# Layer 1's attention: stacks of even and odd heads on the two halves of the partitions, and their score products issued in twos

## The reference

```
q = x @ Wq; k = x @ Wk; v = x @ Wv            # 16 heads; 4 heads; 4 heads
q = rope(q); k = rope(k)
scores = einsum('bhqd,bhkd->bhqk', q, k) / sqrt(D)
p = softmax(scores); o = einsum('bhqk,bhkd->bhqd', p, v)
x = x + o @ Wo + slots_ffn(xn)                # slots: top-8 routing of 64 slots, a GRU step, slot values
```

## Time and profile before

| | us |
|---|---|
| median of 3 executions | 3566.41 (3564.4 to 3569.42) |
| profiled execution, its own time | 3567.51 |
| its span, first to last instruction | 3565.8 |
| TensorE busy | 3229.5 (91%) |
| VectorE busy | 1783.8 (50%) |
| ScalarE busy | 1356.0 (38%) |
| mean granted TensorE clock | 0.933 of full |

### The profile page before, as it was taken

How to read it: one execution, slowest core, us unless ns; L and a number is a source line. 1 busy time by engine, 2 the same in 40 slices (tenths; PEclk the granted TensorE clock), 3 DMA queues, 4 the chain that set the end, 5 groups by cost and what they waited for, 6 DMA issues and landing times.

```text
span 3565.8 us, 51313 instructions
## 1 busy us (share of the span) xinstructions
PE 3229.5 (91%) x15366; PEld 1977.2 (55%) x15367; DVE 1783.8 (50%) x3626; ACT 1356.0 (38%) x1937; POOL 378.9 (11%) x413
## 2 busy tenths in 40 slices
PE   6999999999998999999999999989998688988988
PEld 3455455545544555555545555447665466766666
DVE  5444444544445777777646555662223543334441
ACT  1533434344342555555543233322232233333333
POOL 1100001010000000000011111110111211111110
PEclk7899899889887999999999999989999799999999
DMA  7323422432402222222340101012212333333330
GB/s 230 102 88 85 125 89 61 124 95 68 129 23 75 57 56 56 56 56 56 87 161 30 45 32 40 31 42 69 100 63 66 87 77 84 83 83 76 80 84 14
DMA packets 133002, 273.03 MB, mean 77 GB/s; under 512 B 19680, under 2 KB 77472, under 8 KB 120896
## 3 DMA queue, kind: packets, MB, share of 16 engines
q1 hardware_dynamic: 120352, 233.29, 23.6%
q0 software_dynamic: 10464, 28.59, 2.7%
q10 hardware_dynamic: 2128, 10.43, 0.8%
HBM read 172.49 MB, written 104.33 MB: 78 GB/s over the span
## 4 chain that ended last, share of the span: by engine, by line
PE 77%; DVE 11%; issue 5%; ACT 4%; DMA 2%; POOL 1%; DVEq 0%; SPq 0%; ACTq 0%; POOLq 0%
PE bank_u L526 7%; PE pair L510 6%; PE bank L464 6%; PE bank L487 5%; PE pair L566 4%; PE pair L687 3%; PE pair L1863 3%; PE bank_m L464 3%; PE pair L2230 3%; PE pair L2603 3%; DVE nmax L850 3%; PE pair L731 2%; PE bank_m L2567 2%; PE bank L2567 2%; PE pair L475 2%
## 5 line engine op out<-in xcount | busy, mean ns | idle before, releaser
L763 ACT ACTIVATE probs<-pair 128x1024 f32<-128x1024 f32 x512 | 505.1, 1022 | 341.4 <-PE pair L510 338.3
L850 DVE TENSOR_REDUCE nmax<-bank 128x1 f32<-128x512 f32 x679 | 449.7, 684 | 260.6 <-PE bank L487 256.9
L526 PE MATMUL bank_u<-probs,vext 128*32 128x512 f32 x2048 | 288.2, 636 | 0.8 <-ACT probs L763 0.5
L850 DVE TENSOR_REDUCE nmax<-bank_m 128x1 f32<-128x512 f32 x345 | 235.9, 684 | 79.8 <-PE bank_m L487 74.3
L510 PE MATMUL pair<-q_a,k_a 98*128 98x512 f32 x512 | 192.4, 483 | 46.4 <-DVEq L905 23.6
L1956 DVE TENSOR_REDUCE nmax<-bank 128x2 f32<-128x512 f32 x177 | 118.2, 688 | 179.2 <-PE bank L1786 131.4
L487 PE MATMUL bank<-k_a,q_a 96*128 96x512 f32 x351 | 185.5, 571 | 9.2 <-DMA k_a<-parts_dram 8.4
L510 PEld LDWEIGHTS pair<-q_a,k_a 98*128 98x128 f32 x512 | 102.7, 224 | 142.2 <-ACT probs L763 62.0
L1895 ACT ACTIVATE probs<-pair 128x896 f32<-128x896 f32 x128 | 117.2, 917 | 143.2 <-PE pair L1804 142.3
L510 PE MATMUL pair<-q,k 98*128 98x512 f32 x512 | 167.7, 410 | 3.4 <-DVEq L1515 3.3
L487 PE MATMUL bank<-k,q 96*128 96x512 f32 x328 | 150.4, 493 | 19.8 <-DMA k<-parts_dram 10.7
(11 more groups left out here) (386 smaller groups left out, 6182.0 us busy)
## 6 DMA issues: line engine op xcount, KB each, us to landing
parts_dram<-parts SPq DMA_DIRECT2D x72, 512.0 KB, 2.8
q_a<-parts_dram SPq DMA_DIRECT2D x32, 512.0 KB, 5.1
k_a<-parts_dram SPq DMA_DIRECT2D x32, 512.0 KB, 6.8
q<-parts_dram SPq DMA_DIRECT2D x64, 256.0 KB, 3.7
xl<-xs SPq DMA_DIRECT2D x31, 512.0 KB
xres<-xs SPq DMA_DIRECT2D x24, 512.0 KB
xs<-xres SPq DMA_DIRECT2D x24, 512.0 KB, 3.0
x_in<-xg SPq DMA_DIRECT2D x74, 128.0 KB, 2.0
```

The costliest lines, as they stand in the source:

```text
L526: ins = nc.tensor.matmul(bank_u[32 * h:32 * h + 32, :], vext[:, kt, kv(g, h), :], probs[:, kt % 2, h * SEQ:(h + 1) * SEQ], start=(kt == 0) ...
L763: nc.scalar.activation(probs[:, kt % 2, hp * 2 * SEQ:hp * 2 * SEQ + n], st.tile(l, name)[:, 0:n], ACT.Exp).then_inc(st.free["act"].sem, 1)
L850: nc.vector.tensor_reduce(nmax[:, g % 2, qt, h:h + 1], sc.tile(l, name)[:], AX, ALU.max, negate=True).then_inc(sc.free["dve"].sem, 1)
```

## The change

Both the query and the key stacks now exist on two halves of the partitions. Even heads' stacks stand on partitions 0 to 47 with their maxima on 48 and 49, odd heads' on 64 to 111 with maxima on 112 and 113, and the keys are loaded to both halves. A product contracts 48 or 50 rows. The maxima's products are issued in twos, an even and an odd head of the same query tile: TensorE first waits for both banks, then issues both, and the second one signals for both. `pe_scores_t` keeps its order, but its two heads now lie on different halves. Zeroing the queries is no longer needed (four MEMSETs of VectorE in `POST0` go). A stack takes eight transfers of SP instead of four, and the load of a group's maxima rows two instead of one. `SHARE1` and `sc_plan1` move one product so that all counts are even. A spare tile keeps the addresses of what follows.

```diff
 def sc_plan1(front, back):
-                    ("back", s_uses(3)[:8] + m_use(2) + s_uses(3)[8:13]), ("front", [("L", "dve")]),
-                    ("back", turn_uses(0) + s_uses(3)[13:] + [("GX", "dve")]),
+                    ("back", s_uses(3)[:8] + m_use(2) + s_uses(3)[8:12]), ("front", [("L", "dve")]),
+                    ("back", turn_uses(0) + s_uses(3)[12:] + [("GX", "dve")]),
...
+        def score_at(l, i):
+            return (2 * (i // (2 * TT)) + i % 2, i // 2 % TT) if LAYER[l] == 1 else (i // TT, i % TT)
...
         def dve_max(dve, l, it, step, g, i):
-            h, qt = i // TT, i % TT
+            h, qt = score_at(l, i)
...
-                if not front:
-                    dve_clear_queries(dve, l, 2)
...
-            sp.dma_start(q_rows(g), m_dram[g].rearrange("(a h) n -> a h n", a=2)).then_inc(m_loaded[g % 2].sem, 16)
+            if LAYER[l] == 1:
+                for side in range(2):
+                    sp.dma_start(q_rows(g, side), m_dram[g].rearrange("(a h s) n -> s a h n", a=2, s=2)[side])\
+                      .then_inc(m_loaded[g % 2].sem, 16)
...
-        q_1 = sb("q_1", [P, GROUPS, GH, SEQ], F32, l1)
+        q_1 = sb("q_1", [P, GROUPS, GH // 2, SEQ], F32, l1)
+        spare_q = sb("spare_q", [P, 8 * SEQ], F32, l1)
...
-            nc.vector.memset(k_1[0:96, :, :], 0.0).then_inc(dve_pre1, 1)
-            nc.vector.memset(k_1[96:98, :, :], 1.0).then_inc(dve_pre1, 1)
+            for side in range(2):
+                nc.vector.memset(k_1[64 * side + 32:64 * side + 64, :, :], 1.0).then_inc(dve_pre1, 1)
...
-        def dve_clear_queries(dve, l, g):
-            dve.wait_ge(*st.filled(l, 0, ("E", g, TT - 1, 1)))
-            nc.vector.memset(q_1[0:96, g, :, :], 0.0).then_inc(queries_clear, 1)
...
-        SHARE1 = [6, 8, 10, 12, 13, 14, 15, 16, 16]
+        SHARE1 = [6, 8, 10, 12, 12, 14, 14, 16, 16]
...
             def pair(g, h):
-                return k_1[0:98, g, :], q_1[0:98, g, h, :]
+                at = h % 2 * 64
+                return k_1[at:at + 50, g, :], q_1[at:at + 50, g, h // 2, :]
+
+            def two_scores(g, first, last):
+                for i in range(first, last, 2):
+                    if i == 0:
+                        pe.wait_ge(*stack_ready(l, it, g))
+                    for j in range(2):
+                        for s in sc.vacated(l, it, ("S", g, i + j)):
+                            pe.wait_ge(*s)
+                    for j in range(2):
+                        h, qt = score_at(l, i + j)
+                        ins = nc.tensor.matmul(sc.tile(l, ("S", g, i + j))[:], q(g, h)[:, qt * P:(qt + 1) * P].bitcast(F32R),
+                                               k(g, h).bitcast(F32R), start=True, stop=True)
+                    ins.then_inc(sc.full.sem, 2)
...
                     def maxima(j):
                         if back if g < 2 else front:
-                            for i in range(cut[j], cut[j + 1]):
-                                pe_scores(pe, l, it, (g + 2) % GROUPS, i, q, k)
+                            two_scores((g + 2) % GROUPS, cut[j], cut[j + 1])
...
-                heads = slice(GH * g, GH * g + GH)
-                sp_stack(sp, l, it, g, 0, q_1[:, g, :, :], DIM, HD, heads)
-                sp_stack(sp, l, it, g, 1, k_1[:, g:g + 1, :], 64, HD, slice(g, g + 1))
+                for side in range(2):
+                    at = 64 * side
+                    sp_stack(sp, l, it, g, 0, q_1[at:at + 48, g, :, :], DIM, HD, slice(GH * g + side, GH * g + GH, 2))
+                    sp_stack(sp, l, it, g, 1, k_1[at:at + 48, g:g + 1, :], 64, HD, slice(g, g + 1))
```

More of the change, by code:

```diff
@@ L347, in build @@
         parts_stored = [sig(f"parts_stored{i}", [(16 * SLOT0.count(i), 0), (16 * (i < 3), 0), 0, (16, 0)], "sync") for i in range(4)]
-        stack_loaded = [sig(f"stack_loaded{g}", [(64, 0), (64, 0), 0, (64, 0)], "sync") for g in range(GROUPS)]
+        stack_loaded = [sig(f"stack_loaded{g}", [(64, 0), (128, 0), 0, (64, 0)], "sync") for g in range(GROUPS)]
         high_ready = sig("high_ready", [(8, 0), (3, 0), 0, (4, 0)], "scalar")
@@ L351, in build @@
         m_stored = sig("m_stored", [(16, 48), (16, 48), 0, (16, 48)], "sync")
-        m_loaded = [sig(f"m_loaded{i}", [(16 - 16 * i, 16 + 16 * i), (16 - 16 * i, 16 + 16 * i), 0, (16 - 16 * i, 16 + 16 * i)], "sync")
+        m_loaded = [sig(f"m_loaded{i}", [(16 - 16 * i, 16 + 16 * i), (32 - 32 * i, 32 + 32 * i), 0, (16 - 16 * i, 16 + 16 * i)], "sync")
                     for i in range(2)]
@@ L371, in max_rows_loaded @@
         def max_rows_loaded(l, it, g):
-            return m_loaded[g % 2].at(l, it, 16 * (g // 2 + 1) if g % 2 else 8 * g)
+            return m_loaded[g % 2].at(l, it, (2 if LAYER[l] == 1 else 1) * (16 * (g // 2 + 1) if g % 2 else 8 * g))
+        def score_at(l, i):
+            return (2 * (i // (2 * TT)) + i % 2, i // 2 % TT) if LAYER[l] == 1 else (i // TT, i % TT)
         def stack_ready(l, it, g):
@@ L939, in dve0 @@
                 if not front:
-                    dve_clear_queries(dve, l, 0)
                     dve_slots(dve, l)
@@ L955, in dve0 @@
                 if not front:
-                    dve_clear_queries(dve, l, 1)
                     dve_slot_gates(dve, l)
                 dve_normalise_heads(dve, l, it, step, 2)
-                if not front:
-                    dve_clear_queries(dve, l, 2)
             maxima(1, 0, 8)
@@ L965, in dve0 @@
             if back:
-                if not front:
-                    dve_clear_queries(dve, l, 3)
                 dve_add_out(dve, l, it)
@@ L1039, in sp_max_rows @@
             sp.wait_ge(*m_stored.at(l, it, 16 * (m_order(l, g) + 1)))
-            sp.dma_start(q_rows(g), m_dram[g].rearrange("(a h) n -> a h n", a=2)).then_inc(m_loaded[g % 2].sem, 16)
+            if LAYER[l] == 1:
+                for side in range(2):
+                    sp.dma_start(q_rows(g, side), m_dram[g].rearrange("(a h s) n -> s a h n", a=2, s=2)[side])\
+                      .then_inc(m_loaded[g % 2].sem, 16)
+            else:
+                sp.dma_start(q_rows(g), m_dram[g].rearrange("(a h) n -> a h n", a=2)).then_inc(m_loaded[g % 2].sem, 16)
         def sp_store_out(sp, l, it):
@@ L1202, in build @@
         N1B = 16 * (len(loads1b) + 1)
-        dve_set1, dve_pre1, queries_clear = sem("dve_set1"), sem("dve_pre1"), sem("queries_clear")
+        dve_set1, dve_pre1 = sem("dve_set1"), sem("dve_pre1")
         layer_left = [sem(f"layer_left{i}") for i in range(3)]
@@ L1224, in sp_setup1b @@
             sp.dma_start(bias_bc[:, 0, :], bc("bo1", DIM)).then_inc(loaded1b, 16)
-            sp.wait_ge(queries_clear, GROUPS)
         def pe_slots(pe, l):
@@ L1305, in q @@
             def q(g, h):
-                return q_1[0:96, g, h, :]
+                at = h % 2 * 64
+                return q_1[at:at + 48, g, h // 2, :]
             def k(g, h):
-                return k_1[0:96, g, :]
+                at = h % 2 * 64
+                return k_1[at:at + 48, g, :]
             def pair(g, h):
-                return k_1[0:98, g, :], q_1[0:98, g, h, :]
+                at = h % 2 * 64
+                return k_1[at:at + 50, g, :], q_1[at:at + 50, g, h // 2, :]
[11 more added lines that the diff above has]
+                    ins.then_inc(sc.full.sem, 2)
             def last_maxima(first, last):
                 if back:
-                    for i in range(first, last):
-                        pe_scores(pe, l, it, 3, i, q, k)
+                    two_scores(3, first, last)
             def project(name, half, weight, width=P, halves=2):
@@ L1630, in dve1 @@
             if back:
-                maxima(3, 9, 13)
+                maxima(3, 9, 12)
             if front:
@@ L1635, in dve1 @@
                 dve_normalise_heads(dve, l, it, step, 0)
-                maxima(3, 13, 16)
+                maxima(3, 12, 16)
             if back:
@@ L1678, in sp1 @@
             sp_rounds(sp, l, it, [(rows(0, DIM, 0, P), parts[:, 0, :, :]), (rows(0, DIM, P, P), parts[:, 1, :, :]),
-                                  (rows(1, 64, 0, 64), k_parts[:])], stack, lambda g: q_1[96:98, g, :, :])
+                                  (rows(1, 64, 0, 64), k_parts[:])], stack, lambda g, side: q_1[64 * side + 48:64 * side + 50, g, :, :])
         full.close()
```

## The result

The changed kernel is slower: 3610.7 us (median of 4 executions, 3591.6 to 3626.4) against 3567.9 (4, 3564.4 to 3571.2), a ratio of 1.012 [1.007, 1.017]. Four more executions, taken later beside other runs of before, have a median of 3606.7, 1.014 [1.011, 1.018]. The prediction was 3565.5, with a range from 3549 to 3590.

A forecast was written before the change was run, and what follows sets the result against it. TensorE streams nearly without a gap, but VectorE's banks set a step's start. Seven turns -6.3, PRE1 +6.6, its stack +1.0, POST0 -1.8, POST1 -0.4 sum to -0.9 us: 3566.6 profiled, median 3565.5, range 3549 to 3590.

The forecast's parts named there:

- the sum: Whole kernel: loop turns, PRE1 and its stack, POST0 and POST1 together change the time by -0.9 us.
- Rival (3): Group 2 of the loop: clock falls as less of the array works; 3577 to 3590 us, chance 0.15.
- rival (2): Loop: weight loads overlap, stack in time; step 2.8 us, a turn gains 2.3; total 3553, chance 0.25.
- Pair side by side: TensorE: two products on the array's two halves take 0.25 us together, against 0.47 before.
- Step: Loop, one weighing to the next: 3.0 us with two pairs, against 3.17 before.
- Turn: One turn of layer 1's loop gains 0.9 us: 1.3 in group 3 less 0.4 for the late stack.
- Borders: Loop: 22 new changes of array shape a turn at 0.2 us each, 4.4 us of TensorE's time.
- Double wait: Each maxima pair waits for two banks; the second is free 0.68 us after VectorE starts the pair's first maximum.
- PRE1: Before the loop, at half clock: a pair of maxima takes 1.73 us against 1.22, +6.6 us in all.
- Stack 0 in the loop: SP's queue: eight transfers land at 1358.7, so the product needing them starts 0.4 us later each turn.
- Rival (4): Array halves don't run side by side: step 3.55 us, loop +36, PRE1 +10; 3609 us, chance 0.10.
- rival (5): Loop: stack 0 lands late, +1.5 us a turn; 3576 us, chance 0.10.

The follow-up runs named there:

- e3_twowait: Kernel before, its maxima's products of 96 rows issued in twos behind a wait for both banks, one signal for both; 3616.9 us, ratio 1.015.
- e11_again: The changed kernel run once more, unaltered, in four later executions: median 3606.7 us, ratio 1.014 to the kernel before.
- e1_rows48: Kernel before, its products contracting 48 and 50 rows on one half of the partitions, one at a time; 3645.0 us, ratio 1.022.
- e8_pool0: e2_single with the four transfers of stack 0's odd half issued by GpSimd's queue instead of SP's; 3607.0 us, ratio 1.012.
- e2_single: Changed kernel, its maxima's products issued singly, each with its own bank wait and signal; halves and eight transfers kept; 3591.9 us, ratio 1.009.

## Why the prediction was wrong

**The failed step is the sum, which costed every turn at the full clock.** The sum was -0.9 us; measured are +24 in the profiled executions and +43 at the medians. It had no term for the clock, and the time at half clock grew: by 99 us in the profiled executions, by about 140 at the medians. Rival (3) did name the mechanism and the place, group 2, but set 0.15 on it with one argument against it, "all turns are at 1.00 now though group 2 waits". That says only that waiting with 98 rows does not lower the clock (e3_twowait shows the same). The prediction's own sign for it, a clock below 1.00 in group 2, is what the trace shows. The size was short as well: one or two stretches of 5 us a turn, against 7 to 14 us at half clock in the last six turns of the profiled run and up to 20 in e11_again.

What a microsecond at half clock costs can be read from turns of one kernel. e1_rows48: 45.3 us for 0.39 x 2 x 134.3 = 105, 0.43 each. The changed kernel: 2.44 for 2 x (0.08 x 89.9 - 0.04 x 87.5) = 7.4, 0.33. e8_pool0's two turns above give 0.32, e2_single's 0.50. (The prediction used 1.7 for 5 us, or 0.34 each.) The mean clock fell from 0.933 to 0.914 at the median: 2 x (0.086 x 3609 - 0.067 x 3566) = 143 us more at half clock, at 0.4 each +57. Measured are +43. So everything else, by this estimate, gave 14 us back, where rival (2), 3553, had 12. With 0.32 to 0.50 it is 3 to 29 us, so the agreement is no proof. That the change would win at a held clock is argued from these numbers, and no run shows it: none held the clock without paying for it.

**The other steps.** *Pair side by side*, 0.25 taken: 0.33 to the next instruction, right in kind and a little short; the weight loads overlap too, which the prediction left open. *Step*: 3.0 predicted, 2.94 to 2.96. *Turn*: -0.9 predicted at the full clock; 87.5 less 7 x 0.4 is 84.7 as an estimate, -2.3, which is rival (2)'s figure. *Borders*: 22 counted at 4.4 a turn, +1.9 in e1_rows48, presumably since VectorE's work covers many. *Double wait*: it costs a turn 4.6 with products one behind the other (e3_twowait). With pairs the step of group 3 is 2.94 with it and without it. Over the whole kernel e2_single's ratio is 0.2 to 0.5% under the changed one's, with intervals that touch; clear is only `PRE1`, 6 us. *PRE1*: two pairs in a row,

```profile
1108.80 0.76 PE L1325 MATMUL bank_m<-k,q 48*128 48x512 f32 x1 [0.88 <-DVE nmax L854]
...
1110.47 0.76 PE L1325 MATMUL bank<-k,q 48*128 48x512 f32 x1 [0.88 <-DVE nmax L854]
```

This is 1.67 a pair against 1.73 predicted. From the first product to the first instruction behind the maxima (L1352; L1338 in the kernel before) it is 29.2 instead of 22.8, +6.4 for +6.6 predicted, and 23.2 with single issue. *PRE1's stack*: +1.0 predicted, it came 2.8 earlier, since the whole chain of splits and stores stands 1.5 earlier in `PRE1` and the loads land sooner. *Stack 0 in the loop*: +0.4 predicted. Counted from the turn's start, the first product of group 0 stands 0.9 later in the turn from 1320.87 and 2.5 later in the quick turns, of which a wait for the stack is 0.6; in e2_single's long turns it is 2.3 and 1.5. *POST0*: -1.8 predicted, -0.4 at its end; the trace of after came to this piece 0.7 later, so the piece itself gave 1.1. *POST1*: -0.4, measured -0.2. Rival (4) is refuted by the timeline, rival (5) happens, with waits of 0.5 to 0.7 us in four of the last six turns, and is small.

## What to carry to other kernels

Work out a matmul change's cost twice, at both levels of the clock, and ask where TensorE waits: an edit that makes products smaller there can lose more through the clock than it saves in work. Compare turns of a loop with the granted clock beside them. A product of 65 rows behaves here like one of 96, one of 64 changes the shape: keep neighbours in one shape, and let two products share a wait only where their consumer is not the bound.

## What the runs showed of the hardware

- At 100% busy TensorE can stay at 1.2 GHz: 66 us without a pause, at 0.51 and then 0.50 of the clock, in e1_rows48. The same work runs at 2.4 GHz in other turns.
- The same loop body took 89.0 and 134.3 us in one execution.
- Two products on the two row halves start within 0.01 us of each other, weight loads included, and the next pair follows 0.33 later.
- 64 rows against 65: +6.0 us a turn at the full clock; a border read singly is 0.19.
